# Gating loop: an earlier fetch of indices and seeds, and VectorE's work on the chunk behind in four parts

## The chip, the cores and the metric

One core of a Trainium2 chip runs the whole program. The metric is device time in microseconds. The kernel before took 2620.75 us (median of three runs, 2616.24 to 2620.89).

## What is computed

The reference is a network block on 32 images of 64 x 16 x 16 values. A group norm and a mixed circulant convolution come first. Then the 8192 tokens (256 per image, 64 wide) pass a graph attention over 80,000 edges. Last comes a mixture of four experts, whose gates come from a second graph of 262,144 edges. The change lies in that last graph, the gating:

```python
h = (x_flat @ W_gat).reshape(M, HEADS, NUM_EXPERTS)          # 4 heads x 4 experts
loops = jnp.arange(M, dtype=edge_index.dtype)
src = jnp.concatenate([edge_index[0], loops])
dst = jnp.concatenate([edge_index[1], loops])
a_src = (h * att_src).sum(-1)
a_dst = (h * att_dst).sum(-1)
e = leaky_relu(a_src[src] + a_dst[dst], 0.2)
e_max = segment_max(e, dst, num_segments=M)
ee = exp(e - e_max[dst])
denom = segment_sum(ee, dst, num_segments=M)
alpha = ee / (denom[dst] + 1e-16)
agg = segment_sum(h[src] * alpha[:, :, None], dst, num_segments=M) + b_gat
# layer norm of agg, mean over heads, top 2 of 4, softmax: the experts' gates
```

For every edge a row of 20 numbers of its source (16 of `h`, 4 of `a_src`) has to be fetched, and maxima and sums run along the edges of one destination.

## The kernel before

The edges are sorted by destination first. Then each of the 128 partitions holds a run of them, and the runs are cut into chunks of 64 edges per partition, 128 x 64 = 8192 edges a chunk. With this data 17 chunks are filled (n_all). Along a chunk, maximum and sums with a decay are scans, whose end states go over to the next chunk.

The source rows of a chunk lie in `hs[b]`, one of two buffers. The first two chunks are fetched whole. Of each later chunk, GpSimd fetches 36 of the 64 columns by one indirect DMA each (`g_gather`, L728). The other 28 (PICKS) come from TensorE, out of a table in SBUF, in seven batches of four columns, m = 0 to 6:

- `pick_keys` (VectorE): eight small operations on the chunk's source indices; after the fourth, the cast at L1953, it sets pick_keys_set.
- `spread` (TensorE, L1043): four matmuls that spread a batch's keys over the partitions, into PSUM.
- `all_keys` (ScalarE, L1273): the cast of that from PSUM to SBUF.
- `one_hot` (VectorE, L1370, eight tensor_scalars of 128 x 512): the one-hot matrices of a batch.
- `pick` (TensorE, L1053, 96 matmuls): one-hot times table. It waits for the one-hots of its batch and for pick_taken of the batch two back.
- `take_picked` (VectorE, L1367 and the reduction L1977): multiplies the product by a mask, which sets pick_taken (L1975), and reduces it into `hs[b]`.

One-hots and products have two buffers each. So the one-hot of batch m + 2 waits for pick m, and stands in VectorE's order right before the take of batch m.

While chunk c is picked, chunk c - 1 (the chunk behind) is worked on. `flags` (VectorE) marks where destinations change. `lay` (ScalarE, L1238 to L1246) lays out seeds and end states; it waits for the flags, the seeds and all gathers of that chunk, and sets g_laid. `maximum` (VectorE) takes a scan (L1908), a sum, a leaky relu (L1912), the scan of the maximum (L1915) and three differences. `weigh` (ScalarE, L1253 to L1259) takes the exponentials. `weighted_sums` (VectorE) multiplies the rows by the weights (L1367, 128 x 1024), which sets g_used, and scans the sums (L1928). `rows` (ScalarE, L1267 and L1268) copies them to `g_rows[b]`, 4 us, and sets g_rows_set. SyncE stores these rows (L694) and loads indices, destinations and seeds of the chunk after next (L696 to L699). GpSimd begins a chunk's gathers when its indices are in and the chunk two back is used.

There is no planner in this loop: each engine runs its own program in the written order, and the semaphores alone tie them. The orders that matter, for the pass in which chunk c is picked:

- TensorE (L1066 on): spread 2, pick 0, spread 3, pick 1, up to spread 6, pick 4; then pick 5, spread 0 of chunk c + 1, pick 6, spread 1 of chunk c + 1. A spread 0 waits for pick_keys_set.
- VectorE (L1999 on): flags; then for m = 0 to 4 one-hot m + 2 and take m, with `maximum` behind m = 1 and `weighted_sums` behind m = 2; then pick_keys and one-hot 0 of chunk c + 1, take 5, one-hot 1 of chunk c + 1, take 6, and two operations on all picked rows.
- ScalarE (L1294 on): the casts 2 to 6 with `lay` behind cast 3, `weigh` behind cast 4 and `rows` behind cast 5; then the casts 0 and 1 of chunk c + 1.

In the text, the first to seventh pick are batches 0 to 6.

Of the kernel before, what the change touches and what calls it, by code (L numbers as in the profile page):

```python
# [224 lines left out]
def build(nc, io, debug=None):  # L225
    with ExitStack() as ctx:
# [120 lines left out]
        first = r.at  # L347
# [16 lines left out]
        c = Region(mid)  # L364
# [189 lines left out]
        def _(sp):  # L554
# [132 lines left out]
            with sp.Fori(1, G_CHUNKS // 2) as it:  # L687
                for b in range(2):
                    with sp.If(it * 2 + b < n_all):

                        sp.wait_ge(g_used, it * 2 + (b - 1))
                        sp.wait_ge(g_rows_set, it * 2 + (b - 1))
                        sp.sem_inc(waits_carried, 1)
                        sp.dma_start(gout_v[bass.ds(it * 2 + (b - 2), 1)].rearrange("c p j f -> (c p) j f"), g_rows[b]).then_inc(g_rows_out[b], 16)  # L694
                        nxt = it * 2 + b
                        sp.dma_start(g_sidx[b], gsrc_v[bass.ds(nxt, 1)].rearrange("c p j -> (c p) j")).then_inc(g_idx_in[b], 16)  # L696
                        sp.dma_start(g_didx[b], gdst_v[bass.ds(nxt, 1)].rearrange("c p j -> (c p) j")).then_inc(g_idx_in[b], 16)
                        sp.dma_start(g_dprev[b], gprev_v[bass.ds(nxt, 1)].rearrange("c p j -> (c p) j")).then_inc(g_idx_in[b], 16)
                        sp.dma_start(ad_seed[b], gseed_v[bass.ds(nxt, 1)].rearrange("c p j f -> (c p) j f")).then_inc(ad_seed_in[b], 16)  # L699

            sp.wait_ge(g_rows_set, n_all)
            sp.sem_inc(waits_carried, 1)
# [432 lines left out]
        def _(act):  # L1135
# [46 lines left out]
            def lay(c):  # L1182

                b = c % 2
                act.wait_ge(a_seed_in[b], c // 2 * 16 + 16)
                act.wait_ge(a_flags, c + 1)
                by_f = q_fm.rearrange("p (f j) -> p f j", j=A_RUN)
                nc.scalar.copy(by_f[:, :, 1:], q_seed[b].rearrange("p j f -> p f j")[:, :, 1:])  # L1188
                nc.scalar.copy(a_go.rearrange("p (f j) -> p f j", j=A_RUN), bc(a_nst[:, None, :], [P, HALF_F, A_RUN]))
                act.wait_ge(kv_in[b], (c // 2 + 1) * 16 * (A_RUN + 1))  # L1190
                nc.scalar.copy(by_f[:, :, 0], q_first[b])
                nc.scalar.copy(a_prod.rearrange("p (f j) -> p f j", j=A_RUN), kv[b][:, :, 0:CH].rearrange("p j f -> p f j")).then_inc(a_laid, 1)  # L1192
                nc.scalar.copy(a_msg[:, 0:CH * A_RUN].rearrange("p (f j) -> p f j", j=A_RUN), kv[b][:, :, CH:].rearrange("p j f -> p f j")).then_inc(a_used, 1)
# [6 lines left out]
            def rows(c):  # L1200

                b = c % 2
                act.wait_ge(a_summed, c + 1)
                if c >= 2:
                    act.wait_ge(a_rows_out[b], c // 2 * 16)
                nc.scalar.copy(a_rows[b].rearrange("p j f -> p f j"), a_sum.rearrange("p (f j) -> p f j", j=A_RUN)).then_inc(a_rows_set, 1)  # L1206
# [63 lines left out]
            def all_keys(it, b, m):  # L1270
                act.wait_ge(pick_spread, chunk_count(it, b, BATCHES, m + 1))
                act.wait_ge(pick_hot_set, chunk_count(it, b, BATCHES, m + 1))
                nc.scalar.copy(pick_all[turn_of(b, m)], ps[turn_of(b, m)][:, 0:BATCH * P]).then_inc(pick_all_set, 1)  # L1273
# [20 lines left out]
            with act.Fori(1, G_CHUNKS // 2 + 1) as it:  # L1294
                for b in range(2):
                    with act.If(it * 2 + b < n_all):
                        all_keys(it, b, 2)
                        all_keys(it, b, 3)
                        lay(it, 1 - b, 1)
                        all_keys(it, b, 4)  # L1300
                        weigh(it, 1 - b, 1)
                        all_keys(it, b, 5)
                        rows(it, 1 - b, 1)
                        all_keys(it, b, 6)
                        with act.If(it * 2 + (b + 1) < n_all):
                            for m in range(2):
                                all_keys(it + b, 1 - b, m)
                    with act.If(it * 2 + b == n_all):
                        lay(it, 1 - b, 1)
                        weigh(it, 1 - b, 1)  # L1310
                        rows(it, 1 - b, 1)
# [36 lines left out]
        def _(dve):  # L1348
# [553 lines left out]
                                     bc(g_dprev[b][:, None, :], [P, G_HEADS, G_RUN]), ALU.is_equal))  # L1902
                ts(g_cut, g_nst, BIG, ALU.mult, -BIG, ALU.add).then_inc(g_flags, 1)

            def maximum(it, b, back, first=False):
                c1 = it * 2 + (b - 2 * back * b + 1)
                dve.wait_ge(g_laid, c1)
                link(it, b, back, V.tensor_tensor_scan(ad_edge, g_nst, ad_fm, 0.0, ALU.mult, ALU.add))  # L1908
                hs_f = hs[b].rearrange("p j f -> p f j")
                x_, e_ = (v.rearrange("p (h j) -> p h j", j=G_COLS)[:, :, 1:] for v in (g_x, ad_edge))  # L1910
                link(it, b, back, tt(x_, e_, hs_f[:, G_HF:], ALU.add))
                link(it, b, back, V.scalar_tensor_tensor(x_, x_, 0.2, x_, ALU.mult, ALU.max))  # L1912
                if not first:
                    dve.wait_ge(g_rows_set, it * 2 + (b - 2 * back * b))
                link(it, b, back, V.tensor_tensor_scan(g_max[:, 1:], g_cut, g_x, 0.0, ALU.add, ALU.max))  # L1915
                tt(g_em, g_x, g_max[:, 1:], ALU.subtract)
                link(it, b, back, tt(g_dm, g_max[:, :-1], g_max[:, 1:], ALU.subtract))
                link(it, b, back, tt(g_dm, g_dm, g_cut, ALU.add))
                dve.sem_inc(g_max_set, 1)

            def weighted_sums(it, b, back):
                dve.wait_ge(g_weighed, it * 2 + (b - 2 * back * b + 1))
                w = (g_weight if back else g_msg[:, G_HF * G_COLS:]).rearrange("p (h j) -> p h j", j=G_COLS)[:, :, 1:]
                link(it, b, back, tt(g_msg[:, 0:G_HF * G_COLS].rearrange("p (h k j) -> p h k j", k=G_EXP, j=G_COLS)[:, :, :, 1:],
                                     hs[b][:, :, 0:G_HF].rearrange("p j (h k) -> p h k j", k=G_EXP),
                                     bc(w[:, :, None, :], [P, G_HEADS, G_EXP, G_RUN]), ALU.mult))
                dve.sem_inc(g_used, 1)
                link(it, b, back, V.tensor_tensor_scan(g_sum, g_keep if back else g_corr_f, g_msg, 0.0, ALU.mult, ALU.add))  # L1928
                dve.sem_inc(g_summed, 1)
                assert g_done[0] == G_STEPS_DVE  # L1930
# [52 lines left out]
                pick_link(it, b, V.tensor_reduce(rows_[:, :, G_HF:], prod_.rearrange("p (j h k) -> p j h k", h=G_HEADS, k=G_EXP), AX_X, ALU.add))  # L1983

            flags(0, 0, 0)
            maximum(0, 0, 0, True)
            weighted_sums(0, 0, 0)
            for grp in range(EXPERTS_FIRST, EXPERTS_EARLY):
                expert_group(grp)
# [9 lines left out]
            with nc.Fori(1, G_CHUNKS // 2 + 1, engines=[mybir.EngineType.DVE], head_slot={mybir.EngineType.DVE: 0}) as it:  # L1999
                for b in range(2):  # L2000
                    with dve.If(it * 2 + b < n_all):
                        p_done[0] = 0
                        flags(it, 1 - b, 1)
                        for m in range(BATCHES - 2):
                            one_hot(it, b, m + 2)
                            take_picked(it, b, m)
                            if m == 1:
                                maximum(it, 1 - b, 1)
                            if m == 2:
                                weighted_sums(it, 1 - b, 1)  # L2010
                        for m in range(2):
                            dve.sem_inc(waits_carried, 1)
                            with dve.If(it * 2 + (b + 1) < n_all):
                                if m == 0:
                                    pick_keys(it + b, 1 - b)
                                one_hot(it + b, 1 - b, m)
                            take_picked(it, b, BATCHES - 2 + m)
                        picked_a_src(it, b)
                        dve.sem_inc(waits_carried, 1)
                        assert p_done[0] == PICK_STEPS  # L2020
                    with dve.If(it * 2 + b == n_all):
                        flags(it, 1 - b, 1)
                        maximum(it, 1 - b, 1)
                        weighted_sums(it, 1 - b, 1)
                        V.tensor_copy(row_tail, g_didx[1 - b][:, G_RUN - 1:G_RUN])
                        dve.sem_inc(waits_carried, 1)
# [179 lines left out]
```

## Time and profile before

| | |
|---|---|
| median of three runs | 2620.75 us |
| the profiled execution's own time | 2618.04 us |
| its span, first to last instruction | 2616.2 us |
| VectorE (DVE) busy | 1874.7 us (72%) |
| GpSimd (POOL) busy | 1719.7 us (66%) |
| TensorE matmuls (PE) busy | 1201.4 us (46%) |
| ScalarE (ACT) busy | 682.7 us (26%) |
| gating loop with picks, chunks 2 to 16 | from about 1724 to 2444 us of the span |

Busy time is what the engine spent in instructions, without waits. The chain of waits follows the work that ended last back from the last instruction; its shares tell which work the end hung on. "PEclk" or granted clock is the share of full speed that TensorE's clock was granted. A line number can be a helper's: L1367 and L1370 are VectorE's two-operand and scalar operations anywhere, L728 is every indirect gather. In a timeline a bracket gives the idle time of the engine ahead of the instruction and who ended it.

### The profile page before, as it was taken

The page shows a single profiled execution, that of the slowest core. Times are in us where ns is not written, and L with a number is a line of the kernel's source. Part 1 is how long each engine was busy: PE and PEld are TensorE (multiplying, and loading weights), DVE is VectorE, ACT ScalarE, POOL GpSimd, SP SyncE. Part 2 cuts the span into 40 slices and gives each one's busy share as a digit, 9 for nine tenths or more (in the row PEclk, how much of TensorE's full clock was granted, in tenths as well). Part 3 has the DMA queues.
Part 4 walks back from the last instruction along what each step waited for, and adds up shares of the span by engine and source line. Part 5 has one row for each costly group of instructions (what it writes and reads, how often), then busy time and mean ns, then how long its engine had stood idle before and what let it go on. Part 6 is the DMA issues. An engine that isn't in the chain of part 4 may idle for free.

```text
span 2616.2 us, 34056 instructions
## 1 busy us (share of the span) xinstructions
PE 1201.4 (46%) x12499; PEld 1006.1 (38%) x12499; DVE 1874.7 (72%) x3127; ACT 682.7 (26%) x696; POOL 1719.7 (66%) x1690
## 2 busy tenths in 40 slices
PE   4874000001110101000003499689889899898486
PEld 2532000001000000000002355379889889898366
DVE  7588596999779998887207600168888888888556
ACT  1010002434353534343300111222222222222221
POOL 0001877777777777777777577777777777777370
PEclk9977555555555555555555555579989999899658
DMA  9500213333232332333321606121221222211101
GB/s 300 201 1 23 72 38 101 110 100 97 83 111 87 102 104 94 100 100 131 108 48 33 94 7 189 24 25 26 26 41 26 25 41 26 40 26 26 29 9 34
DMA packets 145714, 186.75 MB, mean 71 GB/s; under 512 B 84844, under 2 KB 103982, under 8 KB 139166
## 3 DMA queue, kind: packets, MB, share of 16 engines
q1 hardware_dynamic: 91494, 121.12, 14.6%
q0 software_dynamic: 54080, 63.61, 12.9%
q8 instruction: 106, 1.74, 0.3%
q14 instruction: 34, 0.28, 0.0%
HBM read 97.32 MB, written 87.32 MB: 71 GB/s over the span
## 4 chain that ended last, share of the span: by engine, by line
POOL 39%; DVE 23%; PE 19%; issue 15%; ACT 1%; SPq 1%; DMA 1%; DVEq 1%; POOLq 0%; ACTq 0%
POOL arena L728 35%; DVE arena L1367 10%; PE psum L1053 9%; DVE arena L1370 7%; PE psum L935 2%; POOL d_adseed L818 2%; DVE arena L1977 2%; DVE arena L1928 2%; PE psum L1014 2%; PE psum L1026 2%; PE psum L904 2%; POOL d_qseed L752 2%; PE psum L1098 1%; SPq L569 1%; PE psum L1129 1%
## 5 line engine op out<-in xcount | busy, mean ns | idle before, releaser
L1367 DVE TENSOR_TENSOR arena<-arena 128x512 f32<-128x512 f32 (+17 forms) x1331 | 766.2, 615 | 210.3 <-DMA arena<-d_ac,arena 65.7
L728 POOL DMA_INDIRECT arena<-d_h,arena x668 | 643.6, 963 | 226.7 <-issue 199.6
L728 POOL DMA_INDIRECT arena<-in_kv,arena x640 | 662.8, 1036 | 195.0 <-issue 195.0
L1053 PE MATMUL psum<-arena 128*128 128x128 bf16 x10080 | 615.7, 225 | 90.2 <-DVEq L1975 88.1
L1053 PEld LDWEIGHTS psum<-arena 128*128 128x128 bf16 x10080 | 602.2, 101 | 95.1 <-DVE arena L1370 91.9
L851 PE MATMUL psum<-arena 128*128 128x128 f32 (+3 forms) x402 | 91.1, 395 | 1021.3 <-DVEq L1443 791.1
L851 PEld LDWEIGHTS psum<-arena 128*128 128x128 f32 (+3 forms) x402 | 69.8, 205 | 1043.8 <-DVEq L1443 806.5
L1370 DVE TENSOR_SCALAR arena<-arena 128x512 bf16<-128x512 f16 (+8 forms) x1067 | 334.1, 371 | 72.6 <-ACT arena L1273 28.8
L1367 DVE TENSOR_TENSOR arena<-psum,arena 128x512 f32<-128x512 f32 (+2 forms) x179 | 141.2, 796 | 210.2 <-PE psum L1014 202.6
L728 POOL DMA_INDIRECT arena<-d_adst,arena x40 | 54.3, 1357 | 257.6 <-DVEq L1614 245.7
L1014 PEld LDWEIGHTS psum<-arena 128*128 128x128 f32 x512 | 113.7, 328 | 146.9 <-issue 110.5
L1768 DVE TENSOR_TENSOR_SCAN psum<-psum,arena 128x1024 f32<-128x1024 f32 x40 | 91.9, 2299 | 82.7 <-ACT arena L1192 81.5
L1014 PE MATMUL psum<-arena 128*128 128x64 f32 x512 | 125.1, 427 | 54.9 <-ACT arena L1279 38.6
L1273 ACT CAST arena<-psum 128x512 f16<-128x512 f32 x105 | 63.1, 602 | 269.6 <-PE psum L1043 264.4
L1026 PE MATMUL psum<-arena 64*128 64x512 f32 x128 | 131.5, 1134 | 0.6 <-ACT arena L1319 0.6
L1188 ACT COPY arena<-arena 128x1984 f32<-128x1984 f32 x20 | 73.1, 3656 | 214.2 <-DMA arena<-d_qseed 147.1
L1206 ACT COPY arena<-arena 128x2304 f32<-128x2304 f32 x20 | 87.9, 4395 | 155.3 <-DVEq L1790 155.3
L1977 DVE TENSOR_REDUCE arena<-arena 128x64 f32<-128x512 f32 x105 | 106.5, 1014 | 15.7 <-DVE arena L1367 7.9
L1367 DVE TENSOR_TENSOR arena<-arena,psum 128x2048 f32<-128x2048 f32 (+4 forms) x47 | 88.5, 1882 | 35.5 <-PE psum L904 28.9
L728 POOL DMA_INDIRECT arena<-d_gs,arena x64 | 67.2, 1049 | 57.0 <-SPq L711 37.8
L1279 ACT ACTIVATE arena<-psum,arena 128x512 f32<-128x512 f32 x64 | 43.7, 688 | 215.9 <-PE psum L1026 215.9
L1788 DVE TENSOR_TENSOR_SCAN arena<-psum,arena 128x1024 f32<-128x1024 f32 x40 | 88.9, 2263 | 0.0
(190 smaller groups left out, 1518.8 us busy)
## 6 DMA issues: line engine op xcount, KB each, us to landing
d_gs<-arena SPq DMA_DIRECT2D x32, 768.0 KB, 4.5
d_as<-arena SPq DMA_DIRECT2D x20, 1152.0 KB, 4.4
d_qseed<-arena SPq DMA_DIRECT2D x5, 4096.0 KB, 29.6
arena<-d_qseed SPq DMA_DIRECT2D x20, 1024.0 KB, 5.1
arena<-d_h,arena POOLq DMA_INDIRECT x668
arena<-in_kv,arena POOLq DMA_INDIRECT x640, 2.5
d_adseed<-arena SPq DMA_DIRECT2D x1, 4096.0 KB, 29.7
arena<-d_adseed SPq DMA_DIRECT2D x17, 128.0 KB
```

What stands on the lines that cost most here:

```text
L728: return pool.indirect_dma_start(out, None, table, bass.IndirectOffsetOnAxis(index[:, t:t + 1], 0))
L851: return nc.tensor.transpose(out, in_, ident[0:n, 0:n])
L1014: last = nc.tensor.matmul(ps[6 + k // 2][:, k % 2 * 256 + e * CH:k % 2 * 256 + (e + 1) * CH], hid[n % 2][:, k * P:(k + 1) * P], w2[:, e, : ...
L1026: nc.tensor.matmul(ps[4 + n % 2][:, :], w1[at, e, :], yT[at, i0:i0 + 4, :].rearrange("p i n -> p (i n)"), start=True, stop=True).then_inc( ...
L1053: last = nc.tensor.matmul(ps[2 + turn_of(b, m)][:, k * PICK_W:(k + 1) * PICK_W], pick_hot[turn_of(b, m)][:, t, k * P:(k + 1) * P], h_split ...
L1188: nc.scalar.copy(by_f[:, :, 1:], q_seed[b].rearrange("p j f -> p f j")[:, :, 1:])
L1206: nc.scalar.copy(a_rows[b].rearrange("p j f -> p f j"), a_sum.rearrange("p (f j) -> p f j", j=A_RUN)).then_inc(a_rows_set, 1)
L1367: return V.tensor_tensor(o, a_, b_, op)
L1370: return V.tensor_scalar(o, a_, s1, s2, op0, op1) if op1 is not None else V.tensor_scalar(o, a_, s1, None, op0)
L1768: step(V.tensor_tensor_scan(q_edge, a_go, q_fm[:, at], 0.0, ALU.mult, ALU.add))
L1788: last = V.tensor_tensor_scan(a_sum[:, at], a_go, a_msg[:, at], 0.0, ALU.mult, ALU.add)
L1977: pick_link(it, b, V.tensor_reduce(hs[b][:, lo:lo + BATCH, 0:G_HF], prod_.rearrange("p j k f -> p j f k"), AX_X, ALU.add))
```

## The change

SyncE, for each later chunk, waits until the chunk two back is laid out (g_laid) and then issues the four loads; only then does it wait for that chunk's rows, and stores them. The wait for g_used is gone. On VectorE, `maximum` is cut into `edge_scores` (L1908 to L1912) and `maximum` (L1915 on), and `weighted_sums` into `messages` (the product) and `weighted_sums` (the scan); the four stand behind the takes of batches 0, 1, 2 and 3. On ScalarE, `lay` moves ahead of cast 3, and cast 6 ahead of `rows`. TensorE's and GpSimd's programs are as before.

```diff
--- before.py
+++ after.py
@@ -688,15 +688,16 @@
                 for b in range(2):
                     with sp.If(it * 2 + b < n_all):
 
-                        sp.wait_ge(g_used, it * 2 + (b - 1))
-                        sp.wait_ge(g_rows_set, it * 2 + (b - 1))
+                        sp.wait_ge(g_laid, it * 2 + (b - 1))
                         sp.sem_inc(waits_carried, 1)
-                        sp.dma_start(gout_v[bass.ds(it * 2 + (b - 2), 1)].rearrange("c p j f -> (c p) j f"), g_rows[b]).then_inc(g_rows_out[b], 16)
                         nxt = it * 2 + b
                         sp.dma_start(g_sidx[b], gsrc_v[bass.ds(nxt, 1)].rearrange("c p j -> (c p) j")).then_inc(g_idx_in[b], 16)
                         sp.dma_start(g_didx[b], gdst_v[bass.ds(nxt, 1)].rearrange("c p j -> (c p) j")).then_inc(g_idx_in[b], 16)
                         sp.dma_start(g_dprev[b], gprev_v[bass.ds(nxt, 1)].rearrange("c p j -> (c p) j")).then_inc(g_idx_in[b], 16)
                         sp.dma_start(ad_seed[b], gseed_v[bass.ds(nxt, 1)].rearrange("c p j f -> (c p) j f")).then_inc(ad_seed_in[b], 16)
+                        sp.wait_ge(g_rows_set, it * 2 + (b - 1))
+                        sp.sem_inc(waits_carried, 1)
+                        sp.dma_start(gout_v[bass.ds(it * 2 + (b - 2), 1)].rearrange("c p j f -> (c p) j f"), g_rows[b]).then_inc(g_rows_out[b], 16)
 
             sp.wait_ge(g_rows_set, n_all)
             sp.sem_inc(waits_carried, 1)
@@ -1295,13 +1296,13 @@
                 for b in range(2):
                     with act.If(it * 2 + b < n_all):
                         all_keys(it, b, 2)
+                        lay(it, 1 - b, 1)
                         all_keys(it, b, 3)
-                        lay(it, 1 - b, 1)
                         all_keys(it, b, 4)
                         weigh(it, 1 - b, 1)
                         all_keys(it, b, 5)
+                        all_keys(it, b, 6)
                         rows(it, 1 - b, 1)
-                        all_keys(it, b, 6)
                         with act.If(it * 2 + (b + 1) < n_all):
                             for m in range(2):
                                 all_keys(it + b, 1 - b, m)
@@ -1902,7 +1903,7 @@
                                      bc(g_dprev[b][:, None, :], [P, G_HEADS, G_RUN]), ALU.is_equal))
                 ts(g_cut, g_nst, BIG, ALU.mult, -BIG, ALU.add).then_inc(g_flags, 1)
 
-            def maximum(it, b, back, first=False):
+            def edge_scores(it, b, back):
                 c1 = it * 2 + (b - 2 * back * b + 1)
                 dve.wait_ge(g_laid, c1)
                 link(it, b, back, V.tensor_tensor_scan(ad_edge, g_nst, ad_fm, 0.0, ALU.mult, ALU.add))
@@ -1910,6 +1911,8 @@
                 x_, e_ = (v.rearrange("p (h j) -> p h j", j=G_COLS)[:, :, 1:] for v in (g_x, ad_edge))
                 link(it, b, back, tt(x_, e_, hs_f[:, G_HF:], ALU.add))
                 link(it, b, back, V.scalar_tensor_tensor(x_, x_, 0.2, x_, ALU.mult, ALU.max))
+
+            def maximum(it, b, back, first=False):
                 if not first:
                     dve.wait_ge(g_rows_set, it * 2 + (b - 2 * back * b))
                 link(it, b, back, V.tensor_tensor_scan(g_max[:, 1:], g_cut, g_x, 0.0, ALU.add, ALU.max))
@@ -1918,13 +1921,15 @@
                 link(it, b, back, tt(g_dm, g_dm, g_cut, ALU.add))
                 dve.sem_inc(g_max_set, 1)
 
-            def weighted_sums(it, b, back):
+            def messages(it, b, back):
                 dve.wait_ge(g_weighed, it * 2 + (b - 2 * back * b + 1))
                 w = (g_weight if back else g_msg[:, G_HF * G_COLS:]).rearrange("p (h j) -> p h j", j=G_COLS)[:, :, 1:]
                 link(it, b, back, tt(g_msg[:, 0:G_HF * G_COLS].rearrange("p (h k j) -> p h k j", k=G_EXP, j=G_COLS)[:, :, :, 1:],
                                      hs[b][:, :, 0:G_HF].rearrange("p j (h k) -> p h k j", k=G_EXP),
                                      bc(w[:, :, None, :], [P, G_HEADS, G_EXP, G_RUN]), ALU.mult))
                 dve.sem_inc(g_used, 1)
+
+            def weighted_sums(it, b, back):
                 link(it, b, back, V.tensor_tensor_scan(g_sum, g_keep if back else g_corr_f, g_msg, 0.0, ALU.mult, ALU.add))
                 dve.sem_inc(g_summed, 1)
                 assert g_done[0] == G_STEPS_DVE
@@ -1983,7 +1988,9 @@
                 pick_link(it, b, V.tensor_reduce(rows_[:, :, G_HF:], prod_.rearrange("p (j h k) -> p j h k", h=G_HEADS, k=G_EXP), AX_X, ALU.add))
 
             flags(0, 0, 0)
+            edge_scores(0, 0, 0)
             maximum(0, 0, 0, True)
+            messages(0, 0, 0)
             weighted_sums(0, 0, 0)
             for grp in range(EXPERTS_FIRST, EXPERTS_EARLY):
                 expert_group(grp)
@@ -2004,10 +2011,8 @@
                         for m in range(BATCHES - 2):
                             one_hot(it, b, m + 2)
                             take_picked(it, b, m)
-                            if m == 1:
-                                maximum(it, 1 - b, 1)
-                            if m == 2:
-                                weighted_sums(it, 1 - b, 1)
+                            if m < 4:
+                                (edge_scores, maximum, messages, weighted_sums)[m](it, 1 - b, 1)
                         for m in range(2):
                             dve.sem_inc(waits_carried, 1)
                             with dve.If(it * 2 + (b + 1) < n_all):
@@ -2020,7 +2025,9 @@
                         assert p_done[0] == PICK_STEPS
                     with dve.If(it * 2 + b == n_all):
                         flags(it, 1 - b, 1)
+                        edge_scores(it, 1 - b, 1)
                         maximum(it, 1 - b, 1)
+                        messages(it, 1 - b, 1)
                         weighted_sums(it, 1 - b, 1)
                         V.tensor_copy(row_tail, g_didx[1 - b][:, G_RUN - 1:G_RUN])
                         dve.sem_inc(waits_carried, 1)
```

## Rows read from the trace of the kernel before

**Rows 1.** Chain of waits, 1800 to 2450 us of the span, by line.
```profile
by line: PE psum L1053 31.7%; DVE arena L1370 22.8%; DVE arena L1367 15.9%; DVE arena L1977 7.7%; issue 6.7%; DVE arena L1928 6.2%; DVE arena L1915 1.5%; DVE arena L1908 1.5%; ACT arena L1273 1.2%; DVE arena L1983 1.2%; PE psum L1043 1.1%; 
```

**Rows 2.** Timeline of TensorE, one pass: start us, us, what, [idle us <- who].
```profile
2130.88 5.52 PE L1053 MATMUL psum<-arena 128*128 128x128 bf16 x96 [1.85 <-DVEq L1975]
...
2140.87 7.15 PE L1053 MATMUL psum<-arena 128*128 128x128 bf16 x96 [4.47 <-DVEq L1975]
...
2147.86 0.39 PE L1043 MATMUL psum<-arena 128*128 128x128 f16 x4
```

**Rows 3.** Timeline of VectorE in the same pass.
```profile
2134.32 2.87 DVE L1928 TENSOR_TENSOR_SCAN arena<-psum,arena 128x1300 f32<-128x1300 f32 x1 [0.15 <-DVE arena L1367]
...
2137.50 2.57 DVE L1370 TENSOR_SCALAR arena<-arena 128x512 bf16<-128x512 f16 x8 [0.31 <-DVE arena L1928]
...
2146.52 0.40 DVE L1370 TENSOR_SCALAR arena<-arena 128x28 int32<-128x28 int32 x2 [0.38 <-DMA arena<-d_gdrow]
...
2147.17 0.18 DVE L1953 CAST arena<-arena 128x28 f16<-128x28 int32 x1
...
2154.48 2.58 DVE L1370 TENSOR_SCALAR arena<-arena 128x512 bf16<-128x512 f16 x8 [1.36 <-ACT arena L1273]
```

**Rows 4.** View of waits, VectorE, 1640 to 2450 us: us, times, longest.
```profile
DVE arena L1370 <- ACT arena L1273: 28.8, 33, 1.5
...
DVE arena L1370 <- DMA arena<-d_gdrow: 9.2, 13, 1.4
```

**Rows 5.** Timeline of TensorE: first picks of chunks 3 and 16.
```profile
1772.39 5.52 PE L1053 MATMUL psum<-arena 128*128 128x128 bf16 x96
...
2392.76 5.41 PE L1053 MATMUL psum<-arena 128*128 128x128 bf16 x94
```

**Rows 6.** Timelines of SyncE and ScalarE.
```profile
2093.27 0.36 SPq L694 DMA_DIRECT2D d_gs<-arena  x1
...
2114.50 0.67 ACT L1238 COPY arena<-arena 128x256 f32<-128x256 f32 x1 [1.85 <-DVE arena L1370]
```

**Rows 7.** GpSimd's gathers, 1800 to 2400 us, by line; and one in the timeline.
```profile
L728 POOL DMA_INDIRECT arena<-d_h,arena x457 | 439.2, 961 | 162.4 <-issue 135.6 <-DMA arena<-d_gdrow 26.8
...
2099.60 0.94 POOL L728 DMA_INDIRECT arena<-d_h,arena  x1 [3.16 <-DMA arena<-d_gdrow]
```

**Rows 8.** Timelines: keys' cast and the seventh pick, first and last of 14 passes.
```profile
1765.82 0.42 DVE L1953 CAST arena<-arena 128x28 f16<-128x28 int32 x1
...
1766.58 5.52 PE L1053 MATMUL psum<-arena 128*128 128x128 bf16 x96
...
2385.74 0.18 DVE L1953 CAST arena<-arena 128x28 f16<-128x28 int32 x1
...
2386.95 5.52 PE L1053 MATMUL psum<-arena 128*128 128x128 bf16 x96
```

**Rows 9.** Timeline of TensorE: the longest sixth pick of 15.
```profile
1900.50 8.18 PE L1053 MATMUL psum<-arena 128*128 128x128 bf16 x96 [4.47 <-DVEq L1975]
```

**Rows 10.** Stretches: us, busy us (count) PE PEld DVE ACT POOL, clock, DMA.
```profile
2088.13:2092.60 4.47, 0.00 (x1) 0.03 (x2) 4.01 (x11) 3.59 (x2) 3.56 (x4) 0.76 0.17 9
...
2092.60:2100.33 7.73, 7.73 (x100) 7.73 (x100) 6.15 (x18) 0.85 (x2) 3.66 (x5) 0.70 0.49 139
...
2128.90:2130.88 1.98, 0.13 (x3) 0.03 (x1) 1.83 (x6) 1.10 (x2) 1.68 (x2) 1.00 0.15 10
```

**Rows 11.** Timeline of VectorE in the pass of chunk 2.
```profile
1737.53 2.46 DVE L1370 TENSOR_SCALAR arena<-arena 128x512 bf16<-128x512 f16 x8 [1.48 <-PE psum L1053]
...
1741.78 0.70 DVE L1908 TENSOR_TENSOR_SCAN arena<-arena 128x260 f32<-128x260 f32 x1
...
1743.24 0.42 DVE L1912 SCALAR_TENSOR_TENSOR arena<-arena 128x256 f32<-128x256 f32 x1
```

**Rows 12.** Timelines of TensorE and VectorE in the last chunk.
```profile
2427.20 13.04 PE L1053 MATMUL psum<-arena 128*128 128x128 bf16 x192 [4.47 <-DVEq L1975]
...
2430.61 0.68 DVE L1367 TENSOR_TENSOR arena<-psum,arena 128x512 f32<-128x512 f32 x1
```

## What I expect of the change

> **What bounds the kernel now.** The page's busy times, in the table above, say that VectorE is busiest, but 72% is an average over stages. So I cut the chain of waits down to the gating loop [rows 1]. GpSimd, which holds 39% of the chain over the whole span, is not among the lines there: TensorE's picks (L1053) hold 31.7%, and the rest is nearly all VectorE (L1370, L1367, L1977, L1928). The loop is a ring of these two engines.
>
> To find where the ring closes I read one pass engine by engine. TensorE makes seven picks for a chunk. The fifth starts after an idle 1.85 us and the sixth after 4.47 us, both held by VectorE's "taken" signal (L1975); then the sixth takes 7.15 us where others take 5.52 [rows 2]. Right behind it stands the first spread of the next chunk, and only then the seventh pick: the program puts that spread between them. In the same pass [rows 3] VectorE finishes the next chunk's keys (the cast, L1953) at 2147.35; TensorE reaches the spread at 2147.86. Two ways to the seventh pick end almost together: VectorE's, through the keys, and TensorE's, through the late and slow sixth pick. Behind the seventh pick come a spread and a cast, and VectorE waits 1.36 us for them before the second one-hot of the next chunk. The sums of the view of waits say the same [rows 4]: 28.8 us in 33 waits for that cast (L1273), and 9.2 us in 13 waits for indices.
>
> **What a pass takes.** The first pick of chunk 3 starts at 1772.39, that of chunk 16 at 2392.76 [rows 5]: 13 passes of 47.72 us. The pass from chunk 2 to 3 and the last chunk are reckoned apart.
>
> **The earlier fetch.** SyncE now waits for the lay-out of the chunk two back instead of its used and stored rows. In the pass shown it issues a store at 2093.27 with the fetches behind it, so its next turn is some 47.7 later, at 2141; the lay-out that it would wait for instead begins at 2114.50 [rows 6]. The fetch comes about 25 us earlier. The DMAs stay five, in another order; behind the new wait stand the four fetches, and behind those the row store, which nobody needs until two chunks later. GpSimd's 26.8 us of waiting for indices goes [rows 7], and is worth nothing: it is not on the chain. Its 36 gathers take 36 x (439.2 + 135.6) / 457 = 45.3 us, which is the end of any pass that falls below it. VectorE's index wait is on the chain: 9.2 us over 13, of which I leave 0.38 each, the wait in the pass of rows 3, for its branch. That gives -0.33 us a pass; its ends are 0 and -0.71.
>
> **The four parts.** The work is the same: two parts become four, each followed by a one-hot that waits. Between instructions that follow at once stand 0.3 us where a scan ends and a one-hot begins (2137.19 to 2137.50), and about as many such gaps go as come: 0, with ends of -0.1 and +0.3. What moves is the scan of 2.87 us (L1928). It stood ahead of the one-hot at 2137.50 and so ahead of the "taken" that starts the sixth pick; now it stands one batch later. The sixth pick starts about 3 us earlier, 1.5 us after the fifth ends instead of 4.47.
>
> That stall does not go away. The keys are made behind the fifth batch; all the VectorE work that stood ahead of them still does. Before, the cast ended 6.48 us after the start of the sixth pick (2140.87 to 2147.35). Now it is 6.48 + 2.87 and a gap of 0.1 more, 9.5 us. The sixth pick ends after 5.52, and the spread waits for the keys: a gap of 4.1 us in TensorE, now ahead of the seventh pick. From the keys on everything is serial: spread, seventh pick, spread, cast, second one-hot.
>
> At best the seventh pick starts 0.34 us after the cast (1766.24 to 1766.58, where TensorE had just finished); over the 13 passes it is 1.03 us on average, the last being 2385.92 to 2386.95 [rows 8]. Now it is 0.34 always: -0.69 a pass. But the slow pick changes places. After the gap of 4.47 us the sixth pick took 7.15 us at the least, 8.18 at the most, 7.79 on average over 15 [rows 2, 9]; VectorE worked beside it and little was lost. The granted clock shows why it was slow [rows 10]: 0.76 in the gap and 0.70 in the pick behind it, so for part of both the engine was at 1.2 GHz, while in the stretch with the short gap it stayed at 1.00, which is 2.4 GHz. In the changed kernel the pick behind the long gap is the seventh, and nothing is done beside it.
>
> A gap of 4.1 us is in no row; the nearest are 4.47 (slow 15 times in 15) and 1.85 (still at 2.4 GHz). I take it as slow, and as it is somewhat shorter I take 7.3 us, in the lower part of the observed durations: 7.3 - 5.52 = +1.78 a pass. The ends are 0 and 8.18 - 5.52 = 2.66.
>
> One rule of the notes speaks against the change. The Trainium skill, page "TensorE: Matmul & The Clock Gate", section "HAM oscillation — how this bites in real kernels", says in substance that a loop which parts its bursts of matmuls by waits drops to the half-rate clock and pays for that in every pass. By it the moved gap makes the seventh pick slow in each pass; by the row of the short gap alone it would not. No gap between these two lengths has been measured here.
>
> **The ScalarE moves.** The lay-out now stands ahead of the fourth cast of keys instead of behind it. Queued behind it are that cast and the one-hot that reads it, which starts 2 us later anyway, behind the first part; and the gather that it waits for had ended 18 us before (2099.60 less 3.16, against 2114.50 [rows 6, 7]). The seventh cast moves ahead of the row copy; the copy then runs beside VectorE's one-hot, take and keys of the sixth pick's stretch, some 6 us. I cost both at 0; without that cover the copy would hold the next chunk's first cast by up to 1 us a pass.
>
> **The sum.** A pass: -0.33 - 0.69 + 1.78 = +0.76, and 13 of them +9.9. The pass from chunk 2 to 3 had no slack behind the keys, but a wait of 1.48 us ahead of its fourth one-hot, which the first part, 1.88 us there (1741.78 to 1743.66), now fills [rows 11]: -1.4 + 1.78 = +0.4. The last chunk makes no keys: its sixth pick starts 3.0 us earlier (2424.2), the seventh needs the fifth batch taken (2430.61 + 0.68, unmoved, + 0.2) and ends at 2437.0 instead of 2440.24 [rows 12]: -3.2. Together +7.1 us. On the profiled execution's own 2618.04 us (a span of 2616.2) that is 2625.1; the median of the three runs lies 2.7 above it, so I forecast 2628.
>
> **The rivals.**
> *The clock holds in the shorter gap* (the other side). A pass is 47.72 - 1.02 = 46.70 us: 13 x -1.02 - 1.4 - 3.2 = -17.9, that is 2603. For it: 4.1 is less than 4.47, and TensorE's other gaps become more even. Against it: the gap that left the clock alone is under half as long. It decides from a seventh pick of 6.8 us (17.9 / 14 above 5.52): below that the kernel is faster.
> *VectorE alone sets the pass.* This is the plain reading of the diff: with the work spread evenly, the waits for the cast go as well (28.8 us over 15 passes less some 0.2 for each wait, 1.5 a pass). A pass is 45.9 us: 13 x -1.83 - 3.2 = -27, about 2594, and GpSimd's 45.3 is just below. Against it: the order in TensorE's queue, which the change does not touch.
> *The slow pick is as bad as the worst now*, 8.18 us in each pass: 13 x 1.64 + 1.3 - 3.2 = +19.4, 2640. For it: the average now, 7.79, gives 2635 already. Against it: the shorter gap.
> *The indices come no earlier,* because the lay-out itself waits for gathers. Then 0.33 a pass is not gained, 2632; the 18 us above speak against it.
>
> **How the numbers follow.** A change of 0.2% (5.2 us) is about what a measurement tells from none. The forecast has 0.60, its own range 2623 to 2637; of that I put 0.36 above 0.2% and 0.24 within it. The clock that holds has 0.21 and VectorE alone 0.05, both faster. The slow extreme has 0.11 and the late indices 0.02, both slower. A mixture of slow and full picks near no change has the last 0.01. So faster 0.26, same 0.25, slower 0.49, and 2600 to 2640 as the range.
>
> **What would show it.** Right: GpSimd's and VectorE's waits for d_gdrow gone; TensorE's longest wait in a pass about 4 us, now ahead of a spread (L1043) and for the keys; the pick behind it over 7 us at a clock below 1; VectorE's wait for the cast (L1273) ahead of the second one-hot up from 1.4 to nearly 3 us. Wrong: that seventh pick at 5.52 us, a sixth pick still held for 4 us, or VectorE without a wait in the pass.

## The result, and the profile after

The changed kernel takes 2625.34 us (median of 8 runs, 2620.16 to 2629.73), the kernel before 2620.38 us on the same chip (8 runs, 2616.24 to 2621.61): a ratio of 1.0022 with a 95% interval from 1.0013 to 1.0032. The ratio is taken over all runs and makes 5.8 us slower, 3.4 to 8.4; the two medians lie 5.0 us apart. The forecast was 7.1 us slower.

The profiled execution took 2628.25 us (span 2626.4), 10.2 us more than that of before. Of this, 6.2 us lie in the gating loop. Another 3.1 us had passed when the loop's first pick began (1727.43 instead of 1724.35), and 0.9 us came behind it; the change touches neither stretch, and the eight runs of the kernel before spread over 5.4 us. Every duration of a pass or a pick here comes from one profiled execution of its kernel.

The chain of waits from 1800 to 2450 us, by line, shows how the ring turned; it answers to [rows 1]:

```profile
by line: DVE arena L1371 29.1%; DVE arena L1368 18.5%; PE psum L1054 14.7%; DVE arena L1982 12.6%; issue 8.9%; DVE arena L1933 6.2%; PE psum L1044 1.5%; DVE arena L1918 1.4%; DVE arena L1909 1.4%; DVE arena L1988 1.3%; ACT arena L1274 1.2%;
```

TensorE's picks (now L1054) fell from 31.7% to 14.7% of the chain, and VectorE took their place. One pick in a pass is left on it, the seventh. TensorE's timeline of one pass (start us, us, what, [idle us <- who]) shows why; it answers to [rows 2]:

```profile
2133.93 5.52 PE L1054 MATMUL psum<-arena 128*128 128x128 bf16 x96 [0.72 <-DVEq L1980]
...
2140.48 5.52 PE L1054 MATMUL psum<-arena 128*128 128x128 bf16 x96 [0.80 <-DVEq L1980]
...
2147.23 5.52 PE L1054 MATMUL psum<-arena 128*128 128x128 bf16 x96 [1.24 <-DVEq L1980]
2157.00 0.61 PE L1044 MATMUL psum<-arena 128*128 128x128 f16 x4 [4.24 <-DVEq L1959]
2157.40 6.60 PE L1054 MATMUL psum<-arena 128*128 128x128 bf16 x96
2163.84 0.61 PE L1044 MATMUL psum<-arena 128*128 128x128 f16 x8
```

The sixth pick (2147.23) waits 1.24 us instead of 4.47 and takes 5.52 us. The long idle time, 4.24 us, now stands one step later, ahead of the spread (L1044), for the keys' signal (L1959). The pick behind it is the slow one. VectorE in the same pass, to be set against [rows 3]:

```profile
2148.24 2.87 DVE L1933 TENSOR_TENSOR_SCAN arena<-psum,arena 128x1300 f32<-128x1300 f32 x1
2151.41 2.52 DVE L1371 TENSOR_SCALAR arena<-arena 128x512 bf16<-128x512 f16 x8 [0.30 <-DVE arena L1933]
...
2156.05 0.40 DVE L1371 TENSOR_SCALAR arena<-arena 128x28 int32<-128x28 int32 x2 [0.38 <-DVE arena L1982]
...
2156.70 0.18 DVE L1958 CAST arena<-arena 128x28 f16<-128x28 int32 x1
...
2164.88 2.51 DVE L1371 TENSOR_SCALAR arena<-arena 128x512 bf16<-128x512 f16 x8 [2.24 <-ACT arena L1274]
```

The scan stands behind the take that starts the sixth pick. The keys' cast ends at 2156.88, the spread starts 0.12 us later, and VectorE waits 2.24 us at its second one-hot of the next chunk until that pick, a spread and a cast are through. Over 13 passes this wait is 2.83 us on average, where the prediction said nearly 3; before it was 1.35. The granted clock of the sixth pick, the gap and the seventh pick (stretch: length, busy us and count of PE, PEld, DVE, ACT, POOL, then clock, DMA share, GB/s), to be set against [rows 10]:

```profile
2147.23:2152.75 5.52, 5.52 (x96) 5.35 (x96) 5.18 (x7) 1.55 (x1) 4.30 (x5) 1.00 0.15 12
2152.75:2157.40 4.65, 0.41 (x6) 0.41 (x5) 3.84 (x12) 2.46 (x2) 3.43 (x5) 0.87 0.36 94
2157.40:2164.00 6.60, 6.60 (x101) 6.60 (x100) 4.83 (x13) 0.59 (x1) 5.08 (x6) 0.83 0.44 67
```

The sixth pick ran at 1.00, which is 2.4 GHz. In the gap and in the seventh pick the clock was for part of the time at 1.2 GHz. The views of waits, 1640 to 2460 us (total us, times, longest), for TensorE, VectorE and GpSimd, to be set against [rows 4, 7]:

```profile
PE psum L1044 <- DVEq L1959: 62.9, 15, 4.4
PE psum L1054 <- DVEq L1980: 38.6, 43, 1.6
...
DVE arena L1371 <- ACT arena L1274: 41.8, 24, 3.7
...
POOL arena L729 <- issue: 192.3, 604, 3.1
POOL arena L729 <- DVEq L1930: 8.6, 4, 3.1
```

No wait for d_gdrow is left on VectorE or GpSimd, and VectorE's wait for the cast grew from 28.8 to 41.8 us.

### The profile page after: what moved, and what is told of

Read it like the earlier page. It is cut to its first block, busy times and chain, and to the rows that moved or that the text cites. A ratio compares the mean times of both kernels' runs of the same rounds, so it can differ in the third digit from the quotient of the medians.

```text
span 2626.4 us, 34071 instructions
## 1 busy us (share of the span) xinstructions
PE 1202.1 (46%) x12499; PEld 1002.8 (38%) x12499; DVE 1876.4 (71%) x3127; ACT 683.7 (26%) x696; POOL 1725.7 (66%) x1690
## 3 DMA queue, kind: packets, MB, share of 16 engines
q8 instruction: 106, 1.74, 0.3%
## 4 chain that ended last, share of the span: by engine, by line
POOL 39%; DVE 28%; issue 16%; PE 13%; ACT 1%; SPq 1%; DMA 1%; DVEq 1%; POOLq 0%; ACTq 0%
POOL arena L729 35%; DVE arena L1368 11%; DVE arena L1371 9%; PE psum L1054 4%; DVE arena L1982 3%; PE psum L936 2%; POOL d_adseed L819 2%; DVE arena L1933 2%; PE psum L1015 2%; PE psum L1027 2%; POOL d_qseed L753 2%; PE psum L1099 1%; SPq L569 1%; PE psum L1130 1%; DVE arena L1918 0%
## 5 line engine op out<-in xcount | busy, mean ns | idle before, releaser
L1054 PE MATMUL psum<-arena 128*128 128x128 bf16 x10080 | 605.2, 223 | 40.6 <-DVEq L1980 38.6
L1054 PEld LDWEIGHTS psum<-arena 128*128 128x128 bf16 x10080 | 591.7, 100 | 47.5 <-DVE arena L1371 40.2
L1371 DVE TENSOR_SCALAR arena<-arena 128x512 bf16<-128x512 f16 (+8 forms) x1067 | 334.1, 371 | 84.2 <-ACT arena L1274 41.8
L1268 ACT COPY arena<-arena 128x1280 f32<-128x1280 f32 x17 | 57.3, 3373 | 172.9 <-DVEq L1934 172.9
```

What stands on the lines that cost most here:

```text
L1054: last = nc.tensor.matmul(ps[2 + turn_of(b, m)][:, k * PICK_W:(k + 1) * PICK_W], pick_hot[turn_of(b, m)][:, t, k * P:(k + 1) * P], h_split ...
L1371: return V.tensor_scalar(o, a_, s1, s2, op0, op1) if op1 is not None else V.tensor_scalar(o, a_, s1, None, op0)
```

## The experiments

Each was compared with the kernel before on the same chip, which took 2617.8 to 2623.7 us there. Ratios are to that kernel. Passes are means of 13, from the first pick of chunk 3 to that of chunk 16: 47.72 us before, 48.37 changed.

**The fetch alone.** Only the SyncE lines of the change.

> Only SyncE's part of the change, all else as before. Theory: in the kernel before, the ring closes through the late sixth pick, which ends 0.1 to 1.5 us after the keys in every pass, so the 0.33 us of waiting for indices lies beside it: no change, 2620 (2618 to 2622), with the index waits of VectorE and GpSimd gone. Rival (the sum of the prediction read literally: the index wait is on the chain by itself): 13 x 0.33 = 4 to 5 us less, 2616.

Measured: 2621.52 us, ratio 0.9994 (0.9985 to 1.0003). VectorE's waits in the loop:

```profile
DVE arena L1371 <- ACT arena L1274: 36.2, 31, 1.5
```

Its 9.2 us of waiting for indices are gone, and 7.4 us more of waiting for the cast stand in their place. By itself the early fetch gains nothing that this measurement can tell: the late and slow sixth pick ends last either way.

**The parts alone.** All of the change but the SyncE lines.

> Only the four parts and ScalarE's order, SyncE as before: it fetches behind the row store. Theory: the scan, and with it the row copy, the store and the fetch, come one batch later, while the keys stay; before, the keys began 9.8 us after the scan's end, with an index wait, and now they could begin 5.1 us after it. So about 4.5 us of index wait in each pass, on the chain, with the seventh pick slow: a pass near 53 us, 2685 to 2695 in all. Rival (the early fetch is worth nothing, as GpSimd is off the chain): as the changed kernel or 4 us above, 2625 to 2630.

Measured: 2685.93 us, ratio 1.0239 (1.0225 to 1.0253). Passes of 52.22 us. VectorE's and TensorE's waits:

```profile
DVE arena L1370 <- DMA arena<-d_gdrow: 57.1, 14, 5.1
...
PE psum L1043 <- DVEq L1958: 114.1, 15, 9.2
```

With the row store at its later time, the indices come up to 5.1 us too late for the keys. So the two halves belong together: without the earlier fetch the parts lose 2.4%, and without the parts the fetch gains nothing.

**The scan put back.** The changed kernel with one thing undone:

```diff
-if m < 4:
-    (edge_scores, maximum, messages, weighted_sums)[m](it, 1 - b, 1)
+if m < 3:
+    (edge_scores, maximum, messages)[m](it, 1 - b, 1)
+if m == 2:
+    weighted_sums(it, 1 - b, 1)
```

> The changed kernel with one thing put back: the scan (weighted_sums) stands again behind the third batch, right behind the messages; edge scores, maximum, the earlier fetch and the ScalarE order stay as changed. Theory (the whole loss is the gap that the scan's move carried from the sixth to the seventh pick): the sixth pick is held for over 4 us again and is the slow one, the seventh takes 5.52 us and the spread ahead of it waits about nothing; the time is that of the earlier fetch alone, 2616 to 2624, ratio to the kernel before 0.998 to 1.001. Rival (the other parts, the split of the maximum or the ScalarE order, cost something by themselves): it stays at 1.002 or more with no gap ahead of the spread.

Measured: 2618.89 us, ratio 1.0004 (0.9995 to 1.0013), passes of 47.78 us. TensorE's sixth and seventh pick of one pass:

```profile
2187.08 8.08 PE L1054 MATMUL psum<-arena 128*128 128x128 bf16 x96 [4.47 <-DVEq L1980]
2195.00 0.38 PE L1044 MATMUL psum<-arena 128*128 128x128 f16 x4
2195.22 5.52 PE L1054 MATMUL psum<-arena 128*128 128x128 bf16 x96
```

Gap and slow pick are back at the sixth pick, and the loss is gone: the intervals of the two ratios only touch, and the passes say it more plainly (47.78 against 48.37). It came from the scan's place. With the scan in its old place, the split of the maximum and the two ScalarE moves cost nothing that this measurement can tell.

**The gap filled.** The changed kernel with 64 matmuls of 128 columns ahead of the spread's wait for the keys; their results are overwritten.

```diff
+pe.wait_ge(pick_all_set, chunk_count(it, b, BATCHES, m + 1))
 if m == 0:
+    for _ in range(64):
+        nc.tensor.matmul(ps[turn_of(b, m)][:, 0:P], h_split[0][:, 0:P], h_split[0][:, 0:P], start=True, stop=True)
     pe.wait_ge(pick_keys_set, it * 2 + (b - 1))
-pe.wait_ge(pick_all_set, chunk_count(it, b, BATCHES, m + 1))
```

> The changed kernel with 64 more matmuls of 128 x 128 ahead of the wait for the keys, into the PSUM bank that the spread then overwrites: nothing is done earlier, TensorE is only kept busy for some 3.6 of the 4.24 us. Theory (the clock): the seventh pick takes 5.52 us instead of 7.09 on average, 13 x -1.57 and -2.3 for chunk 2: 2602. Rival (only the serial chain counts, or the pick is slow for another reason): 2625, or some us more if the added matmuls end after the keys.

Measured: 2641.62 us, ratio 1.0071 (1.0057 to 1.0084): slower, which nothing I had expected explains. TensorE behind two successive chunks:

```profile
2012.24 5.52 PE L1056 MATMUL psum<-arena 128*128 128x128 bf16 x96
2017.60 0.39 PE L1046 MATMUL psum<-arena 128*128 128x128 f16 x4
2021.37 0.39 PE L1046 MATMUL psum<-arena 128*128 128x128 f16 x4 [3.38 <-issue]
2021.60 0.63 PE L1056 MATMUL psum<-arena 128*128 128x128 bf16 x6
2024.17 7.32 PE L1056 MATMUL psum<-arena 128*128 128x128 bf16 x90 [1.93 <-issue]
...
2059.84 3.74 PE L1043 MATMUL psum<-arena 128*128 128x128 bf16 x64
2064.28 0.40 PE L1046 MATMUL psum<-arena 128*128 128x128 f16 x4 [0.70 <-DVEq L1961]
2064.51 5.52 PE L1056 MATMUL psum<-arena 128*128 128x128 bf16 x96
```

Each seventh pick took 5.52 us, as the theory of the clock asks. But in every second chunk, where the loop of two chunks jumps back to its start, TensorE stood 3.38 and 1.93 us with no other engine named (3.0 to 3.4 and 1.9 to 2.4 in the seven such chunks), and the first pick there ran in part at 1.2 GHz. From one seventh pick to the next, passes alternated between some 46.4 and 52.3 us; from first pick to first pick their mean is 49.39. The loop was 128 matmuls longer, so the next run filled the same time with fewer.

**The gap filled by 16 wide matmuls** of 512 columns instead.

> The changed kernel with the gap ahead of the keys filled by 16 matmuls of 512 columns (their results are overwritten) where the run with 64 matmuls of 128 columns had every second pass held by two idle stretches of TensorE of some 3.2 and 1.9 us behind the loop's jump. Theory (the gap's price is the half clock alone, and those stretches come with the 128 more instructions in the loop): no granted clock below 1 in the loop, each seventh pick 5.52 us, passes of 46.3 to 46.8 us instead of 48.37 all alike, 2597 to 2606 us, ratio 0.990 to 0.995. Rival 1 (any extra work ahead of the spread costs what the first fill cost): 2635 to 2645, with the idle stretches there again. Rival 2 (the slow pick isn't from the idle gap): seventh pick still over 6.6 us, 2622 to 2630.

Measured: 2603.55 us, ratio 0.9943 (0.9929 to 0.9956), passes of 46.86 us. One pass of TensorE:

```profile
2225.09 5.52 PE L1056 MATMUL psum<-arena 128*128 128x128 bf16 x96 [1.24 <-DVEq L1982]
2230.45 3.61 PE L1043 MATMUL psum<-arena 128*128 128x512 bf16 x16
2235.04 0.40 PE L1046 MATMUL psum<-arena 128*128 128x128 f16 x4 [0.97 <-DVEq L1961]
2235.27 5.52 PE L1056 MATMUL psum<-arena 128*128 128x128 bf16 x96
```

And the whole loop (length, busy us and count of PE, PEld, DVE, ACT, POOL, clock, DMA share, GB/s):

```profile
1730.00:2428.00 698.00, 641.50 (x10656) 603.60 (x10653) 614.69 (x1339) 179.87 (x263) 516.95 (x535) 1.00 0.23 30
```

The keys come as late as before, and TensorE did work that nobody uses. Yet each seventh pick takes 5.52 us, the long idle stretches of the first fill are gone, and the time against the changed kernel is 0.992 (0.9943 / 1.0022; with the ends of both intervals 0.990 to 0.994). A pass is 1.51 us shorter, close to the 1.57 by which the seventh pick was slow. So the gap's price is the lower clock behind it; the wait itself is still there.

**Half of the gap filled,** by 8 wide matmuls.

> The changed kernel with 8 instead of 16 matmuls of 512 columns ahead of the keys: half of the gap of 4.2 us is filled, some 2.3 us of it stay. It asks about the prediction's first rival (the clock holds in a somewhat shorter gap) at a length between the two rows of the kernel before, 1.85 us (full clock) and 4.47 us (slow). Theory (a gap of 2.3 us behaves as that of 1.85 us): seventh pick 5.52 us in most passes, passes near 46.9 us, 2600 to 2608 us, ratio 0.992 to 0.996. Rival (it behaves as the gap of 4.2 us): seventh pick 6.6 us or more in most passes, passes of 48 us or more, 2618 to 2628 us.

Measured: 2616.61 us, ratio 0.9991 (0.9981 to 1.000), passes of 47.76 us: between the two expectations. Two seventh picks:

```profile
2193.40 0.40 PE L1046 MATMUL psum<-arena 128*128 128x128 f16 x4 [2.62 <-DVEq L1961]
2193.63 7.15 PE L1056 MATMUL psum<-arena 128*128 128x128 bf16 x96
...
2338.11 0.40 PE L1046 MATMUL psum<-arena 128*128 128x128 f16 x4 [2.52 <-DVEq L1961]
2338.34 5.52 PE L1056 MATMUL psum<-arena 128*128 128x128 bf16 x96
```

Of 14 seventh picks behind such a gap, nine took 6.78 to 7.15 us and five 5.52 us. Gaps of 2.62 and 2.52 us gave both, and the two longest, 2.68 us, gave 5.52. So the gap's length alone does not decide; what does was not found.

**The rows ahead.** The changed kernel with ScalarE's copy of rows again ahead of the seventh cast.

```diff
-all_keys(it, b, 6)
 rows(it, 1 - b, 1)
+all_keys(it, b, 6)
```

> The changed kernel with one ScalarE move undone: the copy of rows stands again ahead of the seventh cast of keys. The prediction costed this move at 0 as changed, and said that it is the copy's place that would matter. Theory (with the scan one batch later, the copy of 3.37 + 0.92 us now starts where the seventh one-hot would, so the cast behind it holds that one-hot by about 4.4 us and with it the keys and the seventh pick): VectorE waits about 4 us for the cast ahead of the seventh one-hot in each pass, passes of 52 to 53 us, 2675 to 2690 us, ratio 1.02 to 1.026. Rival (the place of the copy is free here as it was in the kernel before): 2622 to 2630.

Measured: 2691.52 us, ratio 1.028 (1.0264 to 1.0297), 1.5 us above the expected range. VectorE's seventh one-hot of a pass:

```profile
2133.87 2.53 DVE L1371 TENSOR_SCALAR arena<-arena 128x512 bf16<-128x512 f16 x8 [4.56 <-ACT arena L1274]
```

Passes of 52.77 us, 4.40 more than in the changed kernel. The move that the prediction costed at 0 is worth that much: in its old place the copy would now hold the one-hot, since the scan that it waits for comes a batch later.

**The keys early.** The changed kernel with pick_keys behind the fourth batch's take, the scan behind the fifth, and ScalarE's copy of rows behind the next chunk's first two casts.

```diff
-if m < 4:
-    (edge_scores, maximum, messages, weighted_sums)[m](it, 1 - b, 1)
+if m < 3:
+    (edge_scores, maximum, messages)[m](it, 1 - b, 1)
+if m == 3:
+    ...
+    with dve.If(it * 2 + (b + 1) < n_all):
+        pick_keys(it + b, 1 - b)
+        ...
+if m == 4:
+    weighted_sums(it, 1 - b, 1)
...
```

> The changed kernel with the next chunk's keys behind batch 3 and the scan behind batch 4 (they change places), and ScalarE's row copy behind the next chunk's first two casts. Theory (from the keys on the pass is serial, and TensorE's gap ahead of them makes it slow): the spread finds its keys, no gap of 4 us, all seven picks at 5.52 us, and VectorE's wait of 2.2 to 3.7 us ahead of the second one-hot goes: a pass of 45.8 us, close to GpSimd's 45.0 to 45.3, 2585 to 2595 in all. Rival (VectorE's order within a pass does not matter, since its work is the same): 2625.

Measured: 2599.86 us (2598.58 to 2601.91), ratio 0.9908 (0.9893 to 0.9923): against the changed kernel 0.989 (0.9908 / 1.0022; with the ends of both intervals 0.986 to 0.991), and the fastest that computes the whole. The time is 5 us above the expected range. TensorE's only waits for another engine in the loop:

```profile
PE psum L1054 <- DVEq L1980: 87.9, 84, 1.8
```

And the loop as one stretch, with its clock:

```profile
1735.00:2424.00 689.00, 598.84 (x10464) 585.39 (x10462) 610.89 (x1338) 179.11 (x266) 522.31 (x538) 1.00 0.23 31
```

No gap is longer than 1.8 us, and the clock stays at 2.4 GHz. From chunk 3 on no wait of VectorE is put down to another engine, only to its own writes. Passes take 46.32 us, all of them VectorE's; the expected time asks for a shorter pass than VectorE's own work took. GpSimd is close behind: its 538 gathers and the 0.3 us ahead of each fill 686 of the 689 us. The same early keys with the old fetch were not tried. By the written orders they could not run: SyncE would fetch the indices only behind rows that VectorE makes after the keys, and the keys need those indices.

**Few gathers, twice:** in the changed kernel, and in the one with the early keys. Both leave out 32 of the 36 gathered columns of each later chunk, so they do not compute the network.

> The changed kernel with 4 instead of 36 gathered columns of each later chunk (32 rows for each partition are left out, old rows stand in their place): it asks what GpSimd's gathers cost the engines beside them. Theory (VectorE's one-hots run at 2.33 to 2.66 us beside gathers and 2.19 without): all one-hots near 2.19 us, VectorE's stretch from the second one-hot to the keys about 1.4 us shorter, the slow seventh pick unchanged at 6.6 to 8.1 us; a pass of 46.6 to 47.2 us, 2602 to 2612 in all, ratio 0.992 to 0.996. Rival (the two short one-hots of the last chunk have another cause, and the gathers are free to the ring): one-hots and time as in the changed kernel, 2625.

> The kernel with the early keys, which is bound by VectorE alone in the loop (2599.9), with 4 instead of 36 gathered columns of each later chunk (the other 32 are left out). Theory (gathers slow VectorE beside them): seven one-hots of 2.33 to 2.60 us go to 2.19, about 1.8 us a pass, all on the path, as VectorE is the bound: passes of 44.3 to 44.8 us instead of 46.36, 2570 to 2580 in all, ratio 0.981 to 0.985. Rival 1 (gathers free): 2598 to 2602. Rival 2 (VectorE is not the bound, TensorE holds the pass near 46): one-hots short, time 2592 or more.

Measured: 2611.64 us, ratio 0.9969 (0.9957 to 0.9981), and 2565.12 us, ratio 0.9791 (0.9776 to 0.9806). VectorE's one-hots, 1800 to 2380 us (count | busy us, mean ns of one of eight), first in the early keys and then with few gathers:

```profile
L1371 DVE TENSOR_SCALAR arena<-arena 128x512 bf16<-128x512 f16 x700 | 217.2, 382 | 25.7 <-DVE arena L1368 11.2 <-DVE arena L1933 7.2 <-DVE arena L1982 4.8
```

```profile
L1371 DVE TENSOR_SCALAR arena<-arena 128x512 bf16<-128x512 f16 x734 | 203.5, 353 | 26.6 <-DVE arena L1368 11.5 <-DVE arena L1933 7.2 <-DVE arena L1982 5.2
```

Each one-hot operation is 29 ns shorter on average. As they overlap, the busy time counts: 310 ns for each before (217.2 / 700), 277 with few gathers (203.5 / 734), 1.8 us for the 56 of a pass. Where VectorE is the bound, a pass falls from 46.32 to 44.29 us, somewhat more than expected. In the changed kernel it falls only from 48.37 to 47.43; the seventh picks there took 7.82 us on average instead of 7.09, which takes 0.73 us of the gain back. Why the clock was at 1.2 GHz for longer there was not shown.

## Why the prediction was right

*The gap moves and is priced at the seventh pick.* Right, and shown: with the scan put back, gap and slow pick are at the sixth pick again, and the wide fill takes the price away. The gap was 4.24 us in the pass above, 4.1 predicted. The pick took 6.60 to 8.06 us, on average 7.09 over 13, where I took 7.3: +1.57 us a pass instead of +1.78. By the rule of the Trainium skill that the prediction weighed ("TensorE: Matmul & The Clock Gate", section "HAM oscillation — how this bites in real kernels"), every pass pays; the trace agrees, 14 of 14. Behind the half-filled gap of 2.5 to 2.7 us it was 9 of 14.

*Cast to seventh pick, 1.03 to 0.34 us.* It is 0.49 on average: in 8 of the 13 passes the spread runs in the slow stretch too, 0.61 us instead of 0.39. So -0.54 instead of -0.69. The two errors of size nearly cancel.

*The index wait, -0.33 a pass.* The fetch comes earlier as predicted: in the pass above SyncE issues it at 2125.26, behind the lay-out, and the store at 2155.45 [rows 6].

```profile
2125.26 0.33 SPq L694 DMA_DIRECT2D arena<-d_gsrow  x1
...
2155.45 0.35 SPq L700 DMA_DIRECT2D d_gs<-arena  x1
```

In sum the term is right too: VectorE's stretch from a chunk's second one-hot to the end of the next keys' cast is 0.38 us shorter, 39.86 instead of 40.24. But the fetch alone gave nothing, as above. The prediction added this term as if it stood by itself, and called the index wait part of the chain; before, it lay beside the late sixth pick. The gain exists only with the moved scan; and left out, it costs not 0.33 but 3.85 us a pass (52.22 - 48.37).

*The ScalarE moves, 0.* Nothing in the trace speaks against it as changed, but the lay-out's move was not undone by itself. For the copy of rows, "up to 1 us a pass" without that cover was about the first cast of the next chunk; the 4.40 us of the undone move sit at the seventh cast, which I did not name.

*The sum.* A pass is +0.65 us, predicted +0.76. From chunk 2 to 3 it was +1.74 instead of +0.4: that seventh pick took 7.85 us, 0.55 above my 7.3, and the loop's first pick, in the slow stretch that precedes the loop, 8.16 instead of 7.55, another 0.61. The last chunk gave -3.99 instead of -3.2; its last two one-hots took 2.19 us each, where earlier ones took 2.33 to 2.66; GpSimd's last gather had ended at 2431.28:

```profile
2433.81 2.19 DVE L1371 TENSOR_SCALAR arena<-arena 128x512 bf16<-128x512 f16 x8 [0.31 <-DVE arena L1368]
...
2440.97 2.19 DVE L1371 TENSOR_SCALAR arena<-arena 128x512 bf16<-128x512 f16 x8 [0.30 <-DVE arena L1933]
```

13 x 0.65 + 1.74 - 3.99 = +6.2 us, against +7.1. The mechanism was right; that the sum came so close is partly luck, as the errors of the pass and those of the two ends each cancel in good part.

*The rivals.* The clock that holds would have given 2603, a ratio of 0.9932, with passes of 46.70 us; filling the gap comes near that case, 0.9943 and 46.86. That its time, 2603.55, is the same figure is chance, as it was taken on another chip. VectorE alone would have given 2594, a ratio of 0.9898 (its sum left out the -1.4 of the pass from chunk 2 to 3); the early keys come near it with 0.9908. Their pass was 46.32 us, not 45.9. I held the order in TensorE's queue against this rival, and rightly for the change as it stands: it evened out VectorE's work but left the keys late for that order. The early keys leave the order as it is and meet it in time.

## What to carry to other kernels

When a wait is taken from one instruction, follow the last producer of the ring (here the keys) and see at which consumer it is late next, with which clock that consumer will run, and what is left beside it to hide it. Here work of VectorE moved by one batch moved a gap from a slow pick that was half hidden to one on which all else waits. Move the late producer itself ahead, rather than the work around it; if it can't be moved, idle time of TensorE ahead of a serial burst may be worth filling, with few and wide matmuls.

## What the runs showed of the hardware that I had not expected

- **The length of a gap alone did not decide the clock.** Behind gaps of 2.51 to 2.68 us picks took 5.52 us five times and 6.78 to 7.15 nine times in the same kernel.
- **VectorE was slower beside many gathers.** With 36 of GpSimd's indirect DMAs a chunk a one-hot operation took 382 ns on average, with 4 of them 353. The Trainium skill, page "SBUF — State Buffer", section "SBUF: two separate sides", says that GpSimd's instructions and some of VectorE's (those in a two-port mode or with two inputs in SBUF) share a pair of ports that one of them holds for a whole instruction. The direction agrees; the size does not look like a block for a whole gather (0.94 us). No run shows the port itself or whether the one-hots use it, and none tells GpSimd's instructions from the DMA traffic that they start.
- **A longer loop came with a TensorE that stood still.** With 128 small matmuls more in the loop there were idle stretches of 3.0 to 3.4 and 1.9 to 2.4 us behind its jump, with 32 wide ones none. That they come from fetching the longer program was not shown.
